# Attention over 56x56 images: seven query chunks of 448 columns in natural order, row maxima reordered, ring of six sums

## The reference

```python
x = x + _L0_conv_ref(_gn(x), L0_conv_weight)     # 3x3 convolution with sign(weight)
t = _to_tokens(x)                                # 3136 tokens of 64 channels
t = t + _L1_attn_ref(_ln_t(t), W_q, W_k, W_v, W_o, b_o)
t = t + _L1_ffn_ref(_ln_t(t), ...)               # 8 experts, gates from the mean over the images
...
Q = jnp.einsum('bsd,du->bsu', inputs, W_q)       # U = 32; K and V alike
attn = jnp.einsum('bqu,bku->bqk', Q, K) * scale
w = jax.nn.softmax(attn, axis=-1)
out = jnp.einsum('bqk,bku->bqu', w, V)
return jnp.einsum('bsu,ud->bsd', out, W_o) + b_o + inputs
```

## Time and profile before

| | us |
|---|---|
| median of 3 runs | 7242.83 (7240.38 to 7246.4) |
| the profiled execution | 7243.7 |
| its span | 7241.9 |
| PE busy | 6983.8 (96%) |
| POOL busy | 5473.8 (76%) |
| DVE busy | 5012.9 (69%) |
| ACT busy | 4372.2 (60%) |

### The profile page before, as it was taken

One profiled execution on the slowest core, in us unless ns is written; L12 is line 12 of the kernel. 1 busy time (PEld: TensorE's weight loads), 2 busy tenths in 40 slices (PEclk: granted clock), 3 DMA queues, 4 the chain that ended last, 5 costly groups with the idle time before them and its releaser, 6 DMA issues. The chain is left out here.

```text
span 7241.9 us, 132870 instructions
## 1 busy us (share of the span) xinstructions
PE 6983.8 (96%) x48626; PEld 3566.1 (49%) x48626; DVE 5012.9 (69%) x9053; ACT 4372.2 (60%) x9329; POOL 5473.8 (76%) x5524
## 2 busy tenths in 40 slices
PE   7999999999999999999999999999999959999999
PEld 4555555555555555555555555555555523333332
DVE  6777777777777777777777777777777714444444
ACT  1666666666666666666666666666666634555555
POOL 2888888888888888888888888888888852222222
PEclk7999999999999999999999999999999979999999
DMA  1011111111111111111111111111111003333333
GB/s 30 15 23 23 23 23 23 23 24 23 23 23 23 23 24 23 23 23 23 23 23 23 23 23 23 23 23 23 23 24 23 10 25 78 80 82 83 84 83 79
DMA packets 324411, 240.54 MB, mean 33 GB/s; under 512 B 253368, under 2 KB 307000, under 8 KB 319808
## 3 DMA queue, kind: packets, MB, share of 16 engines
q1 hardware_dynamic: 311616, 208.17, 12.9%
q0 software_dynamic: 12288, 25.71, 1.6%
HBM read 156.30 MB, written 77.48 MB: 32 GB/s over the span
## 5 line engine op out<-in xcount | busy, mean ns | idle before, releaser
L611 ACT ACTIVATE probs<-bank 128x392 f32<-128x392 f32 x6400 | 2797.0, 496 | 1887.1 <-PE bank L658 1849.9
L478 DVE TENSOR_REDUCE part_max<-bank 128x1 f32<-128x448 f32 x5600 | 3211.6, 613 | 583.6 <-PE bank L651 574.6
L651 PE MATMUL bank<-ks,qs 96*128 96x448 f32 x5600 | 2347.4, 424 | 55.4 <-DVE part_max L478 50.0
L425 POOL TENSOR_TENSOR psum<-psum,probs 128x392 f32<-128x392 f32 x2048 | 2100.4, 1026 | 320.5 <-ACT probs L611 34.0
L422 POOL TENSOR_TENSOR psum<-probs 128x392 f32<-128x392 f32 x2048 | 2100.6, 1026 | 236.7 <-ACT probs L611 224.4
L658 PE MATMUL bank<-qs,ks 97*128 97x392 f32 x6400 | 2026.3, 367 | 15.2 <-ACT probs L611 12.8
L667 PE MATMUL bank<-probs,vs 128*32 128x392 f32 x12288 | 1765.4, 506 | 37.2 <-POOL psum L425 28.1
L669 PE MATMUL bank<-psum,ones 128*32 128x392 f32 x4096 | 1737.8, 506 | 0.0
L651 PEld LDWEIGHTS bank<-ks,qs 96*128 96x128 f32 x5600 | 1065.5, 190 | 1230.4 <-DVE part_max L478 746.0
L658 PEld LDWEIGHTS bank<-qs,ks 97*128 97x128 f32 x6400 | 1190.9, 190 | 405.5 <-ACT probs L611 222.3
L1007 DVE SCALAR_TENSOR_TENSOR h<-ebank,tmp_n,gate_w 128x784 f32<-128x784 f32 x512 | 529.2, 1034 | 644.2 <-PE ebank L1060 644.2
(11 more groups left out here) (127 smaller groups left out, 5336.1 us busy)
## 6 DMA issues: line engine op xcount, KB each, us to landing
xin<-in_x_dram SPq DMA_DIRECT2D x64, 784.0 KB, 8.9
xs<-x_dram SPq DMA_DIRECT2D x512, 98.0 KB, 2.4
xpk<-in_x_dram SPq DMA_DIRECT2D x64, 392.0 KB, 12.7
t_dram<-t SPq DMA_DIRECT2D x32, 784.0 KB, 5.1
x_dram<-xn SPq DMA_DIRECT2D x32, 784.0 KB, 6.6
res<-t_dram SPq DMA_DIRECT2D x256, 98.0 KB, 2.5
out_dram<-fin POOLq DMA_DIRECT2D x256, 98.0 KB, 2.5
row_dram<-row_max SPq DMA_DIRECT2D x192, 2.0 KB
```

Source lines behind the costliest of these rows:

```text
L425: add = gp.tensor_tensor(into, into, three, ALU.add)
L478: v.tensor_reduce(part_max[:, b, m:m + 1], m_bank[place.bank()][:, 0:MW], AX.X, ALU.max).then_inc(m_used, 1)
L611: s.activation(probs[:, held(c, k), :], s_bank[n % 3][:, 0:2 * QW], ACT.Exp, scale=SCALE).then_inc(p_ready, 1)
L651: mm(m_bank[place.bank()][:, 0:MW], qs[par][0:KS, b * P:(b + 1) * P], ks[par][0:KS, m * MW:(m + 1) * MW], start=True, stop=True).then_inc( ...
```

## The change

- QC is 7 and QW 224: a chunk is 448 columns, an image has 175 scores instead of 200, 56 value rounds instead of 64, and SLOT is 168 units.
- `qs` holds the queries in their natural order, like `ks`. A score reads its chunk as two runs of 224 columns, one from each half. The writes of the projected queries are plain runs.
- The blocks for the maxima are taken in the order `BLOCK_OF`: two of the first half and the two of the second half with the same places, and so on, block 24 last. So row r serves chunk r, and `rows_needed(c)` is c + 1. The row's second DMA writes two runs of 256 columns.
- SUMS is 6; the rings of `probs`, `psum` and score banks run on over the images instead of starting anew, since 168 is no multiple of 16 and 56 none of 6.
- The places are new. VISIT_AT is -3.38, so value round n stands at 3n + 12.62.

```diff
-QC = 8
+QC = 7
...
-HELD, SUMS = 16, 8
+HELD, SUMS = 16, 6
...
-VISIT_AT, DOOR = 0.0, 1
-SUM_LAG, APPLY_LAG = 1.22, 3.72
-GATHER_AFTER, DIVIDE_AFTER, DIVIDE_STEP = -0.19, 0.1, 0.73
-STATS_AT, STATS_STEP, PAD_AT, PAD_STEP = 93.6, 2.18, 117.81, 17.71
+VISIT_AT, DOOR = -3.38, 1
+SUM_LAG, APPLY_LAG = 1.55, 2.46
+GATHER_AFTER, DIVIDE_AFTER, DIVIDE_STEP = -0.11, 0.1, 0.5
+STATS_AT, STATS_STEP, PAD_AT, PAD_STEP = 71.26, 1.06, 103.22, 11.75
...
-BORDER, LAST_MAX = 58.0, 9.34
-ROW_AFTER = (1.2, 4.1)
-FETCH_AT, STORE_AT = 60.89, 113.0
+BORDER, LAST_MAX = 50.76, 8.77
+ROW_AFTER = (7.6, 8.8)
+FETCH_AT, STORE_AT = 53.34, 99.69
...
-    return -(-(c + 1) * 2 * QW // (P * MR))
+    return c + 1
+BLOCK_OF = [b + d for b in range(0, KB // 2, 2) for d in (0, 1, KB // 2, KB // 2 + 1)] + [KB - 1]
...
-ACT_LAG = 0.9
+ACT_LAG = 0.14
...
-        def held(c, k):
-            return (c * BLOCKS + k) % HELD if k < BLOCKS else HELD
+        def held(im, c, k):
+            return im.count(SLOT, c * BLOCKS + k) % HELD if k < BLOCKS else HELD
...
-            if n < 2:
-                return tile[part, 0:S].rearrange("p (c a i) -> p c a i", a=2, i=QW)[:, q * CW // QW:(q + 1) * CW // QW, n, :]
-            return tile[part, (n - 2) * HALF + q * CW:(n - 2) * HALF + (q + 1) * CW]
+            return tile[part, n % 2 * HALF + q * CW:n % 2 * HALF + (q + 1) * CW]
...
-                        wait(pe, p_ready, im.count(QC * KB, c * KB + k - 2 if c or k > 1 else k - 1))
-                        mm(s_bank[(c * KB + k) % 3][:, 0:2 * QW], ks[par][0:KS + 1, k * P:(k + 1) * P], qs[par][0:KS + 1, c * 2 * QW:(c + 1) * 2 * QW],
+                        n = im.count(QC * KB, c * KB + k)
+                        wait(pe, p_ready, n - 2)
+                        queries = qs[par][0:KS + 1, 0:S].rearrange("p (a n) -> p a n", a=2)[:, :, c * QW:(c + 1) * QW]
+                        mm(s_bank[n % 3][:, 0:2 * QW].rearrange("p (a n) -> p a n", a=2), ks[par][0:KS + 1, k * P:(k + 1) * P], queries,
```

More of the change, by code:

```diff
@@ L70 @@
 VALUE_AFTER = HELD - VISIT
-VISIT_AT, DOOR = 0.0, 1
-SUM_LAG, APPLY_LAG = 1.22, 3.72
-GATHER_AFTER, DIVIDE_AFTER, DIVIDE_STEP = -0.19, 0.1, 0.73
-STATS_AT, STATS_STEP, PAD_AT, PAD_STEP = 93.6, 2.18, 117.81, 17.71
-PREPARE_AT = (0.4, 2.6, 5.3, 7.6, 19.2, 19.9, 25.4, 28.1, 30.6, 32.6, 35.9, 38.6)
-NORMS_AT = (69.7, 74.5, 77.8, 81.9, 92.7, 95.9, 101.3, 106.5)
-PROJ_AT, PROJ_STEP = 12.23, 3.3
-VALUES_AT = (50.8, 58.0)
-BORDER, LAST_MAX = 58.0, 9.34
-ROW_AFTER = (1.2, 4.1)
-FETCH_AT, STORE_AT = 60.89, 113.0
+VISIT_AT, DOOR = -3.38, 1
+SUM_LAG, APPLY_LAG = 1.55, 2.46
+GATHER_AFTER, DIVIDE_AFTER, DIVIDE_STEP = -0.11, 0.1, 0.5
+STATS_AT, STATS_STEP, PAD_AT, PAD_STEP = 71.26, 1.06, 103.22, 11.75
+PREPARE_AT = (0.4, 2.3, 4.1, 6.6, 18.0, 20.6, 21.1, 24.6, 26.8, 28.5, 31.4, 33.7)
+NORMS_AT = (60, 64.6, 67, 70.4, 77.1, 80, 83.7, 88.6)
+PROJ_AT, PROJ_STEP = 14.04, 3.82
+VALUES_AT = (40.9, 44.5)
+BORDER, LAST_MAX = 50.76, 8.77
+ROW_AFTER = (7.6, 8.8)
+FETCH_AT, STORE_AT = 53.34, 99.69
 def visit_at(n):
@@ L370, in step @@
                         blocks = slice(r * MR, min((r + 1) * MR, KB))
-                        n0, n1 = blocks.start * P, min(blocks.stop * P, S)
                         sp.wait_ge(rowmax_ready, im.count(NMR, r + 1))
@@ L375, in step @@
                         sp.wait_ge(row_bounced, im.count(16 * NMR, 16 * r + 16))
-                        sp.dma_start(qs[par][KS:KS + 1, n0:n1].bitcast(F32), row_dram[par:par + 1].rearrange("a b p -> a (b p)")[:, n0:n1]).then_inc(row_ready[r], 16)
+                        b, row = BLOCK_OF[blocks.start], qs[par][KS:KS + 1, :].bitcast(F32)
+                        if b + 1 == KB:
+                            to, of = row[:, b * P:S], row_dram[par, blocks, 0:S - b * P]
+                        else:
+                            to = row[:, 0:(KB - 1) * P].rearrange("o (h n) -> o h n", h=2)[:, :, b * P:(b + 2) * P]
+                            of = row_dram[par:par + 1, blocks, :].rearrange("a (h b) p -> a h (b p)", h=2)
+                        sp.dma_start(to, of).then_inc(row_ready[r], 16)
                     elif kind == "store":
@@ L418, in step @@
                         first, rounds = c * KB + GROUP * r, c * ROUNDS + r
-                        one, two, three = (probs[:, held(c, GROUP * r + n), :] for n in range(GROUP))
-                        into = psum[:, rounds % SUMS, :]
+                        one, two, three = (probs[:, held(im, c, GROUP * r + n), :] for n in range(GROUP))
+                        into = psum[:, im.count(QC * ROUNDS, rounds) % SUMS, :]
                         gp.wait_ge(p_ready, im.count(QC * KB, first + 2))
@@ L521, in step @@
                             dst, src = proj_cols(which, part, q, n), m_bank[place.bank()][part, 0:CW]
-                            if n < 2:
-                                src = src.rearrange("p (c i) -> p c i", i=QW)
                             dve.wait_ge(part_hi, im.count(4 * CH, 4 * q + n + 1))
@@ L608, in step @@
                         c, k = a
-                        n = c * KB + k
-                        act.wait_ge(s_done, im.count(QC * KB, n + 1))
-                        s.activation(probs[:, held(c, k), :], s_bank[n % 3][:, 0:2 * QW], ACT.Exp, scale=SCALE).then_inc(p_ready, 1)
+                        n = im.count(QC * KB, c * KB + k)
+                        act.wait_ge(s_done, n + 1)
+                        s.activation(probs[:, held(im, c, k), :], s_bank[n % 3][:, 0:2 * QW], ACT.Exp, scale=SCALE).then_inc(p_ready, 1)
                     elif kind == "gather":
@@ L650, in step @@
                         wait(pe, m_used, place.m(place.use + 1 - MB))
-                        mm(m_bank[place.bank()][:, 0:MW], qs[par][0:KS, b * P:(b + 1) * P], ks[par][0:KS, m * MW:(m + 1) * MW], start=True, stop=True).then_inc(m_done, 1)
+                        mm(m_bank[place.bank()][:, 0:MW], qs[par][0:KS, BLOCK_OF[b] * P:(BLOCK_OF[b] + 1) * P], ks[par][0:KS, m * MW:(m + 1) * MW], start=True, stop=True).then_inc(m_done, 1)
                     elif kind == "score":
@@ L666, in step @@
                             for n in range(GROUP):
-                                mm(o_bank[n * U:(n + 1) * U, 0:2 * QW], vs[par][:, GROUP * r + n, :], probs[:, held(c, GROUP * r + n), :],
+                                mm(o_bank[n * U:(n + 1) * U, 0:2 * QW], vs[par][:, GROUP * r + n, :], probs[:, held(im, c, GROUP * r + n), :],
                                    start=r == 0, stop=False)
-                            mm(o_bank[GROUP * U:P, 0:2 * QW], ones[:], psum[:, (c * ROUNDS + r) % SUMS, :], start=r == 0, stop=r + 1 == ROUNDS)
+                            mm(o_bank[GROUP * U:P, 0:2 * QW], ones[:], psum[:, im.count(QC * ROUNDS, c * ROUNDS + r) % SUMS, :], start=r == 0, stop=r + 1 == ROUNDS)
                         if TURN * g + TURN == ROUNDS:
```

## The result

The changed kernel takes 7306.71 us (median of 4 runs, 7301.09 to 7315.51) where the kernel before takes 7244.61 (4 runs, 7240.38 to 7247.24). The ratio is 1.0087, 95% interval 1.007 to 1.0105: 62 us slower. The forecast was 7187, with a range of 7115 to 7255. The profiled execution of after took 7302.88 us, its span is 7301.2.

A forecast was written before the change was run, and what follows sets the result against it. POOL's work plus its rest was taken to set an image's length: 168.6 + 7.6 + 2.0 = 178.2 us, 1.75 less than 179.95. Over 32 images that is 56 us, giving 7187 us, range 7115 to 7255.

The forecast's parts named there:

- The rest: Ring of sums, rows of maxima, row DMAs, ACT and DVE: no wait; prologue, tail and expert phase unchanged within a few us.
- PE's own work: TensorE's work per image falls by 3.4 us: 2.7 from value rounds, 0.3 from scores, 0.4 from small f32 matmuls.
- the 2.7 us: PE's saving per image from 56 value rounds instead of 64, 64.6 us becoming 61.8 us.
- The 0.3 us of the scores: PE's saving per image from 175 wider scores instead of 200; stated ends 0 and 1 us.
- The 0.4 us for small f32 matmuls: PE's saving per image where means, variances or projections stand beside other f32 work, 0.11 us per change back.
- POOL's add: GpSimd's add grows from 392 to 448 columns, costing 0.123 us more; POOL's work 168.6 us per image, ends 165.9 and 171.5.
- rival 2: POOL sets the pace from the fourth chunk on: 7280 us, or 7248 with half the lead's 2 us kept; chance 28%.
- The lead: POOL's time from score to value falls from 11.4 to 9.45 us; PE waits 1.6 us more per image for sums.
- The formula: An image lasts POOL's work, 168.6 us, plus its rest, 7.6 us and 2.0 us of lost lead: 178.2 us.
- Rival 1: The shorter lead suffices, so PE's own saving counts: 176 to 176.6 us per image, 7117 to 7136 us; chance 24%.
- Rival 3: Two-run query reads cost PE 0.01 us per score, 1.7 us per image: about 7240 us; chance 3%.
- the closer pads: POOL's four pad steps, closer and earlier, cost the same 7.9 us: nothing in the sum, though waits may begin a chunk earlier.

The follow-up runs named there:

- e9: Changed kernel with BORDER at 51.7 instead of 50.76, so one value round comes ahead of the first maximum: 7243.56 us, ratio 1.0002.
- e3: Kernel before with PROJ_AT at 16.1 instead of 12.23, the last projection right ahead of the first maximum: 7318.73 us, ratio 1.01.
- e12: Changed kernel with the projections earlier (PROJ_AT, PROJ_STEP 10.7, 2.89 instead of 14.04, 3.82), BORDER unmoved: 7304.11 us, ratio 1.0083.
- e1: Changed kernel with BORDER at 54.7 instead of 50.76, the next image's maxima beginning three units later: 7212.36 us, ratio 0.9959.
- e11: e1 with the pads 15.5 units apart instead of 11.75: 7211.52 us, ratio 0.996 against the kernel before.
- e10: e1 with APPLY_LAG at 3.72, as before the change, instead of 2.46: 7220.43 us, ratio 0.9971 against the kernel before.
- e6: e1 with POOL's pad subtraction cut to 1 of its 14 rows: 7177.44 us, ratio 0.991 against the kernel before.
- e4: Kernel before, eight chunks kept, with the natural order of queries, two-run score reads and new order of maxima: 7244.16 us, ratio 0.9999.
- e2: e1 with VISIT_AT at -1.0 instead of -3.38, value rounds 2.38 units later: 7682.18 us, ratio 1.0604 against the kernel before.
- e5: e2 with the second normalization's places (NORMS_AT) also moved 2.38 units later: 7462.46 us, ratio 1.0311 against the kernel before.
- e8: Changed kernel with the kernel before's table of places, scaled by 168/192, some moved against collisions, value rounds at 3n + 16: 7456.37 us, ratio 1.0297.

## Why the prediction was wrong, point by point

**The step that failed: "The rest".** This paragraph goes through the ring of sums, the rows of the maxima, the DMAs, ACT and DVE, and says "No wait." The wait of an image's first maximum for the corrected `ks` is in none of the prediction's terms; it was put at nothing without a reason. The places of the border are in the diff and in the table (BORDER from 58.0 to 50.76), and the prediction costed what the move does to the density of the maxima and not what it does to their first one. The working that was missing is short: last projection at 33.7 + 14.04 + 3.82 = 51.56 units, first maximum at 51.58, before 54.13 and 58.10. Between them lies a chain of ACT and DVE that every image needs, 2.6 us from the projection's start to the maximum (3138.54 to 3141.16). The slack of 4 units had covered it. In the runs this wait took 1.7 us per image and the clock behind it 1.2. e9 shows that moving the border by one operation is worth 63 us, all of the loss. Of the 3.6 us between the image forecast (178.2) and the one measured (181.8) the clock is about 1.2, PE's idle time 1.3 (the 1.7 for `ks`, less for maxima), and PE's saving, taken too large, 1.2.

**The clock: 1.2 us per image, never thought of.** The prediction read the clock row as a constant. That did not hold: 1.70 us of idle at the border was followed by a fall in 21 of 31 images; 0.8 us at the border (e3, e9) never; and 0.56 us at another place in 6 of 30 (e12). Within the one trace the images fall in classes, the first one aside: 180.3 to 180.7 us without a fall (10 images), 181.8 to 182.2 with 3.4 us at the lower clock (9), 183.3 to 183.4 with 6.8 us (9). That sets the price of a fall at 1.5 and 2.9 us, with nothing else changed.

**PE's own work: 3.4 forecast, 2.2 measured.** The passes of a value round step 0.41 us (3689.20, 3689.61) where 0.40 was worked out, so the 2.7 us stand. The 0.3 us of the scores did not come: a score of 448 columns steps 0.20 to 0.21 us (3690.40, 3690.60) and takes as long as the maximum beside it, so 175 of them cost what 200 at 0.18 did; that was inside the stated ends. The 0.4 us for small f32 matmuls came with the other sign. By line, in 4,000 us, projections, means and variances of 22 images took 473.3 us on PE before and 481.8 after, 0.4 us more per image (486.2 in e1, where the clock never fell); 2.7 - 0.4 is 2.3. They moved next to other f32 work, and no saving is to be seen.

**POOL's add: 1.149 forecast, 1.142 measured.** The middle between proportion (1.173) and the pad's slope (1.126) was right, and rival 2's point of decision, 1.164, was not reached. The slope is 0.116 us for 56 columns. The prediction's estimate from the 2.6 cycles per element that the Trainium skill gives for a two-input add, in "GPSIMD Engine Reference", section 3.1, was 0.121, and the trace agrees within 0.005.

**The lead: waits for sums 30 to 50 us in 4,000 forecast, 48.5 measured.** The step held in the changed kernel: 1.7 us more per image where 1.6 was said. But it is no constant of the shorter lead. With the maxima moved (e1) it is 22.3, and with the pads apart (e11) none, at the same time. Taking the same work from POOL was worth 1.0 us per image with seven chunks and 0.6 with eight, so POOL's grip on the time grew by some 0.4 us and not by 1.6 once the border was right. That bears on all that changed for POOL together. By itself the lead could not be tested.

**The formula.** "An image lasts POOL's work plus its rest" gave 178.2. With the border put right the image lasts 178.85, which is near, but in part by luck: PE's saving was over-sized by 1.2 us and the lead's price over-sized too, and the errors cancelled in part. The rest was no constant either. The prediction had 7.6 us, and 9.6 after the change. POOL's recorded waits are 173.4 us in 4,000 before, 7.8 per image, and 317.0 after, 14.4 per image. Of these 4.1 are a wait for the inverse deviations at the applies (L443) which the kernel before does not have there; the new APPLY_LAG brings it, since most of it goes with the old value (e10), and the prediction carried the applies over unchanged. And e6, with 5.7 us less work for POOL, gives only 1.0 us back. So POOL's work plus a fixed rest does not set the length of an image.

**The rivals.** Rival 1 (the lead suffices) was wrong for the kernel, and even e6, where PE waits for no sum, stays above its 176 to 176.6 us with 177.9. Rival 2 had the right side for the wrong reason: its signs would have been an add near 1.173 us and over 100 us of waits for sums in 4,000, and neither is there. Rival 3 is refuted by e4. That the closer pads put nothing in the sum was right, by e11. None of the rivals was a wait that the new places create, though three of the experiments (e2, e5, e8) show how many such places there are. That is likely also why the chance of slower, 0.14, was too low.

**What stays open.** Why the same 1.70 us brings a fall in two images of three and none in the third, and why 0.56 us does in e12 in one of five. Where e12's longer busy time comes from. What the lead is worth alone. And why e1's waits for sums are free by e11, while less work for POOL is worth 35 us by e6 (7212.36 to 7177.44): something in POOL's pace must count besides the waits that PE is recorded to have for it, and it was not found. It is not the wait at the applies, by e10.

## What to carry to other kernels

When a change moves places in a hand-written order, list for each wait of the busiest engine its producer's old and new distance, above all for first uses that wait for everything of an earlier stage; a distance that falls from four units to none can be a cost, whatever the diff is about. A gap of the matrix engine that recurs in every turn can have two prices, its length and what the clock does behind it, so it is worth moving one independent operation into it. Judge a recorded wait by taking its cause away, not by its length: waits for sums of 1 us per image went at no gain here (e11), and halving one of 1.7 us gave back 1.8 us, 1.2 of it from the clock (e9).

## What the runs showed of the hardware

- 1.70 us of recorded idle of TensorE, in a stretch in which it was otherwise busy, was followed by 3.4 or 6.8 us at 1.2 GHz in 21 of 31 images. At the same place 0.8 us never was (e3, e9), but 0.56 us between two projections was in 6 of 30 (e12), and two waits of 0.72 and 0.59 us close together once, by 10.2 us (e9). So the runs show no length of gap that is safe everywhere. All four runs of the changed kernel had a mean granted clock of 0.973 to 0.976, those of e9 0.981 to 0.983.
- A moving operand in two runs of 196 columns costs a matmul nothing that can be measured: 7244.16 us against 7244.07, ratio 0.999 to 1.0009 (e4).
- GpSimd's two-input add of f32 on 128 partitions costs 2.07 ns per further column (1.026 to 1.142 us for 56), from which I estimate 0.21 us for no columns.
